# Layer phase: GpSimd's rotation behind VectorE's, value sums two head pairs at a time, statistics and second parts moved to the residual

## The reference, cut to what matters

```python
xn = _layernorm(x, axis=-1)
# first block: 16 heads of 16, segments of 512 tokens, keys and values of every eighth token
q, k, v = (qkv[0] * scale, qkv[1], qkv[2])
scores = jnp.einsum('bhspd,bhskd->bhspk', q4, k4).reshape(B, H, S, nb, BLOCK_M, Kn)
c = jnp.max(scores, axis=4, keepdims=True)
w = jnp.exp(scores - c)
den = jnp.sum(w, axis=-1) + 1e-10
out = jnp.einsum('bhsnmk,bhskd->bhsnmd', w, v4) / den[..., None]
s = out @ Wout.T
g = _silu(quantised(xn) @ weight.T + bias)
x = x + s * g
# second block
xn = _layernorm(x, axis=-1)
q = rope(xn @ wq + bq); k = rope(xn @ wk + bk); v = xn @ wv + bv
# causal attention per head, then a mixture of 8 experts as the gate, x = x + s * g
```

## Time and profile before

| what | value |
|---|---|
| the profiled execution's own time | 3820.8 us |
| span of its instructions | 3819.0 us |
| median of the three timed runs | 3812.4 us |
| busy share of the span: PE, DVE, ACT, POOL | 85%, 72%, 52%, 17% |
| mean granted TensorE clock, share of full speed | 0.92 |
| iterations 2 to 14 of the layer phase, 148.81 to 886.18 | 737.4 us |

### The profile page before, as it was taken

One profiled execution on the slowest core, in us unless ns is written; L12 is line 12 of the kernel. 1 busy time (PEld: TensorE's weight loads), 2 busy tenths in 40 slices (PEclk: granted clock), 3 DMA queues, 4 the chain that ended last, 5 costly groups with the idle time before them and its releaser, 6 DMA issues. The chain is left out here.

```text
span 3819.0 us, 67859 instructions
## 1 busy us (share of the span) xinstructions
PE 3249.5 (85%) x22678; PEld 1773.4 (46%) x22679; DVE 2754.2 (72%) x5118; ACT 2004.4 (52%) x3363; POOL 651.7 (17%) x954
## 2 busy tenths in 40 slices
PE   5878878877398898899899899999979899999977
PEld 2434434434133333333333333333348788888865
DVE  5777777776778888788788888888725565555547
ACT  2333333333057777788788788788852232222224
POOL 1132222222122232000000000000023323223310
PEclk9999999998579999999999999999989999999989
DMA  2122222222422211222222112220031121111149
GB/s 72 50 71 67 61 67 67 61 67 67 86 43 46 45 19 32 47 46 45 47 46 45 21 31 46 46 46 18 17 108 63 39 78 44 59 54 45 45 131 332
DMA packets 252770, 230.55 MB, mean 60 GB/s; under 512 B 60924, under 2 KB 235132, under 8 KB 252156
## 3 DMA queue, kind: packets, MB, share of 16 engines
q1 hardware_dynamic: 236040, 192.39, 19.9%
q0 software_dynamic: 16384, 33.64, 2.8%
HBM read 124.28 MB, written 101.06 MB: 59 GB/s over the span
## 5 line engine op out<-in xcount | busy, mean ns | idle before, releaser
L1474 ACT ACTIVATE at_ex<-at_so,keep_exp_scale 128x512 f32<-128x512 f32 (+1 forms) x2304 | 1350.6, 673 | 447.9 <-PE at_so L1368 241.4
L1501 DVE TENSOR_REDUCE at_best<-at_p 128x1 f32<-128x512 f32 (+3 forms) x2560 | 1393.3, 603 | 261.4 <-PE at_p L1350 162.9
L1350 PE MATMUL at_p<-at_ks,at_qs 48*128 48x512 f16 (+3 forms) x2560 | 811.4, 370 | 165.6 <-DVE at_best L1501 123.7
L1368 PE MATMUL at_so<-at_qs,at_ks 50*128 50x512 f16 (+3 forms) x2560 | 694.5, 362 | 18.7 <-issue 9.5
L1422 PE MATMUL at_ob<-at_ex,at_vs 128*32 128x512 f32 (+3 forms) x5120 | 608.3, 567 | 0.5 <-issue 0.4
L1772 ACT ACTIVATE e_hh<-e_hb,e_b1now 128x512 fp32r<-128x512 f32 x256 | 174.5, 690 | 595.5 <-PE e_hb L1707 541.6
L1657 POOL DMA_INDIRECT e_xg<-s_xn,e_token x128 | 143.4, 1121 | 1695.7 <-DVE e_token L1802 1523.8
L1350 PEld LDWEIGHTS at_p<-at_ks,at_qs 48*128 48x128 f16 x2560 | 216.9, 94 | 459.3 <-DVE at_best L1501 393.1
L1368 PEld LDWEIGHTS at_so<-at_qs,at_ks 50*128 50x128 f16 x2560 | 200.1, 95 | 464.6 <-ACT at_ex L1474 346.4
L1737 PE MATMUL e_ob<-e_w2h,e_hh 128*128 128x256 f32 x1024 | 298.5, 292 | 15.7 <-DVE e_og L1840 15.1
L1738 PE MATMUL e_ob<-e_w2l,e_hh 128*128 128x256 f32 x1024 | 294.4, 288 | 0.0
(11 more groups left out here) (209 smaller groups left out, 4651.6 us busy)
## 6 DMA issues: line engine op xcount, KB each, us to landing
s_v<-a_v SPq DMA_DIRECT2D x64, 256.0 KB, 3.2
s_qk<-a_part SPq DMA_DIRECT2D x128, 128.0 KB, 2.4
at_vs<-s_v SPq DMA_DIRECT2D x32, 512.0 KB
s_eo<-at_empty SPq DMA_DIRECT2D x16, 1024.0 KB
e_w<-w SPq DMA_DIRECT2D x16, 1024.0 KB
f_rows<-s_eo SPq DMA_DIRECT2D x32, 512.0 KB, 8.4
at_qs<-s_qk SPq DMA_DIRECT2D x96, 128.0 KB
at_ks<-s_qk SPq DMA_DIRECT2D x96, 128.0 KB
```

The lines of the kernel that those rows point to most:

```text
L1350: last = pe.matmul(out, qs[rows, buf, p, qt * P:(qt + 1) * P], ks[rows, buf, p, ch * SEG:ch * SEG + w], start=True, stop=ch != qc)
L1368: last = pe.matmul(so[:, v % NST, at:at + w], ks[rows, r, p, kt * P:(kt + 1) * P], qs[rows, r, p, q0:q0 + w], start=True, stop=not diag)
L1474: ev.done(act.activation(ex[:, v % NE, 0:width], so[:, v % NST, 0:width], ACT.Exp, scale=keep["exp_scale"][:, 0:1]), "ex")
L1501: ev.done(dve.tensor_reduce(best[:, row:row + 1, ch], p1[:, (at + e) % NP1, 0:wide(item)], AX, ALU.max), "mx")
```

## The change

POOL's rotation waits for the end of DVE's rotation of the same segment instead of for the copies of q and k. PE's order in the pair loop is changed: the values of two pairs follow each other behind the second scores of the next two, each value waits for the exponentials of both pairs, and `wexp` has four buffers instead of two. ACT's copies to `oT` come one pair later, the first part at p = 6 instead of 3. On DVE `normalise` comes two pairs later, the second part `rest` and the statistics of the next x leave the pair loop: the statistics stand behind the second `gated`, then the multiplication of the gate, then `rest`, then the tokens xn of the next segment, then the remaining part of the residual. The number of instructions of each kind is the same.

```diff
+        NW = 4
-        wexp = sb("wexp", [P, 2, SEG])
+        wexp = sb("wexp", [P, NW, SEG])
@@ gpsimd, rotate
-                    ev.wait(pool, "pjc", n, 4)
+                    ev.wait(pool, "rot", n, 1)
@@ tensor, values
-                    ev.wait(pe, "wexp", m, p + 1)
+                    ev.wait(pe, "wexp", m, p + 2 - p % 2)
-                    ev.done(pe.matmul(ob[r:r + 2 * HW, :], vbd[:, p, :], wexp[:, p % 2, :], start=True, stop=True), "pv")
+                    ev.done(pe.matmul(ob[r:r + 2 * HW, :], vbd[:, p, :], wexp[:, p % NW, :], start=True, stop=True), "pv")
@@ tensor, the pair loop
-                        if p >= 1:
+                        if p >= 2 and p % 2 == 0:
+                            values(m, p - 2)
                             values(m, p - 1)
-                        if p >= 3 and p % 2 == 1:
-                            turn(m, (p - 3) // 2)
+                        if p >= 4 and p % 2 == 0:
+                            turn(m, (p - 4) // 2)
+                    values(m, NP0 - 2)
                     values(m, NP0 - 1)
+                    turn(m, 2)
                     gate(m, 0)
@@ scalar, the pair loop
-                        ev.wait(act, "pv", m, max(p - 1, 0))
-                        ev.done(act.activation(wexp[:, p % 2, :], shifted[:, p % 2, :], ACT.Exp, scale=SCALE), "wexp")
+                        ev.wait(act, "pv", m, max(p - NW + 1, 0))
+                        ev.done(act.activation(wexp[:, p % NW, :], shifted[:, p % 2, :], ACT.Exp, scale=SCALE), "wexp")
-                        if p == 3 and n >= 1:
+                        if p == 6 and n >= 1:
                             part0(n - 1)
-                        if p >= 2 and p % 2 == 0:
-                            out_copy(m, p // 2 - 1)
+                        if p >= 3 and p % 2 == 1:
+                            out_copy(m, (p - 3) // 2)
@@ vector, residual
-                def residual(st, m):
-
-                    ev.wait(dve, "ez", m, 2)
-                    st.mark(dve.scalar_tensor_tensor(out=z[:], in0=ez[:], scalar=1.0, in1=z[:],
-                                                     op0=ALU.add, op1=ALU.mult), "gate", m)
-                    st.settle()
+                def residual(st, m, half):
+
+                    if half == 0:
+                        ev.wait(dve, "ez", m, 2)
+                        st.mark(dve.scalar_tensor_tensor(out=z[:], in0=ez[:], scalar=1.0, in1=z[:],
+                                                         op0=ALU.add, op1=ALU.mult), "gate", m)
+                        return
+                    ev.wait(dve, "gate", m, 1)
@@ vector, the loop
-                        if p == 4 and n >= 1:
-                            rest(st, n - 1)
-                        if p >= 3 and p % 2 == 1:
-                            normalise(st, m, (p - 3) // 2)
-                        if p == 5 and more:
-                            normed_tokens(st, m + 1, 0)
+                        if p >= 5 and p % 2 == 1:
+                            normalise(st, m, (p - 5) // 2)
+                    normalise(st, m, 2)
                     gated(st, m, 0)
                     normalise(st, m, 3)
                     gated(st, m, 1)
                     if more:
+                        normed_tokens(st, m + 1, 0)
+                    residual(st, m, 0)
+                    if n >= 1:
+                        rest(st, n - 1)
+                    if more:
                         normed_tokens(st, m + 1, 1)
-                    residual(st, m)
+                    residual(st, m, 1)
                     second_norm(st, m, 0)
```

## The result

The changed kernel takes 3871.5 us (median of four runs, 3867.5 to 3880.2), the kernel before in the same comparison 3814.7 (3809.0 to 3821.1): a ratio of 1.0148 with an interval of 1.0125 to 1.0171. So it is 57 us slower, clear of the noise, where 100 were forecast; 3871 lies inside the range, 41 under the predicted number. The profiled execution of after took 3867.5 with a span of 3865.7.

What follows compares the result with a forecast made beforehand. Neither PE (82% busy) nor DVE (75%) was full, so the order of waits decides. 33.6 + 29.4 = 63.0 against 56.7 an iteration, +82 over 13; with iteration 15, tail and first iterations +100: 3912 us, range 3845 to 3950.

Steps and rivals of the forecast that it cites:

- POOL's operations block the four normalisations, in turns: Start of an iteration: POOL's three rotations alternate with the four L768; xn1 ready at 8.1 instead of 2.7.
- A: Rival at the iteration start: the four L768 keep the port together; +3.1 an iteration, +51 in total; chance 0.13.
- B: Rival at the iteration start: L768 free, L789 and L791 blocked; +1.6 an iteration, +28 in total; chance 0.10.
- C: Rival: nothing at the iteration start blocks; -1.4 or -0.7 an iteration, -14 or -4 in total; chance 0.11.
- two values 2.0: Pair loop: the value matmuls of two pairs take 2.0 on PE within a round of 6.4.
- the 32.9 of the prediction: Pair loop: the first gate matmul starts 32.9 into the iteration, before half pace is added; 26.7 before the change.
- the 0.7: Gate: added to its start time for half pace behind a 2.8 gap before values 6, making 33.6.
- the second stall: Behind the gate: Newton steps on POOL are shut out, xn comes late, PE stands 3.2 before its transpose.
- D: Rival: half pace on PE behind its 3.2 stall, 1.5 more each time, +20 to +40; upper edge of forecast's 0.60.
- taking them out of the loop gains nothing there: Pair loop: moving out L871 (2.29) and the statistics (2.4) gains nothing; the round's own chain fills the time.
- the third part: Statistics and second parts moved to the residual: 3.2 of the 3.8 gained on the rotation given back there.
- the tail: End of the layer phase: +6.4 for the last block's xn1 and +7.1 for POOL's last rotation following DVE's.

## Why the prediction was right in its sign and off in its size

**Right: POOL's operations block the four normalisations, in turns.** Shift 1 came at 7.7 into the iteration (forecast 8.0), xn1 at 7.7 (8.1), PE's gap was 5.2 (5.6), and half pace followed it. L768 was taken as a blocked form by its neighbour L703; rivals A (it goes in one piece) and B, C (it is free) fell with the 6.42. The four begin at 207.29, when L330 is half done, and the last of them ends at 213.71, half a microsecond behind POOL's L333 (213.25): 5.05 more than the 1.37 that they take alone, for three operations of POOL's.

**Wrong: "two values 2.0".** The term of the round that I priced by one pair, doubled. One pair is 1.04 and two are 1.08. It entered four times. Values 0 and 1 took 1.98 at half pace, not 3.8; the scores behind them ran at half pace too and gave part of that back, so values 2 came at 16.5, not 17.75 (0.3 of it because xn1 was ready earlier). From there to the gate 12.9 passed, not 15.2. So the gate came 3.5 earlier than the 32.9 of the prediction; the 0.7 that I added to the 32.9 is there, but inside the gate (2.24 against 1.47). With the two forced apart values 2 came at 17.76 and the rounds were 6.43. The rest of the round was sized rightly, and the rounds of 5.27 are made of it.

**Wrong by the part that I had given to a rival: the clock behind the second stall (D).** The stall itself came as worked out: statistics, two-input work on DVE, the Newton step behind L877, xn 2.96 late, PE 3.09 (forecast 3.2). Behind it the transposes took 1.66 where they take 1.04 at full pace, and L500 3.04 where it takes 1.88: +1.8 an iteration. I had 0.60 on the forecast with D as its edge; in all thirteen iterations of after it is simply part of it. Together: 63.0 - 3.5 + 1.8 = 61.3, the iteration of the trace. That the total came within 41 us of the forecast is in part luck, since these two errors have opposite signs. Nor is the 1.8 a fixed price: with the values forced apart a stall of 3.11 at the same place was followed by full pace in one iteration (1.09 and 1.88, at 395.89) and by half pace in the next (1.97 and 2.40, at 460.23).

**The mean is lower, 60.9, by two iterations.** Those that start at 390.00 and 693.69 are 58.3 long. The same gap of 2.75 precedes their last values, and these and the gate run at full pace (granted clock 1.00):

```profile
415.69 1.08 PE L444 MATMUL a_ob<-a_wexp,a_vbd 128*64 128x512 f32 x4 [2.75 <-ACT a_oT L583]
...
417.19 1.47 PE L462 MATMUL a_pb<-a_wf_piece,a_xq 128*128 128x256 bf16 x12
```

So a gap of 2.75 was followed by half pace in some iterations (1.52 and 2.24 in the fence above) and not in others, and the two kinds differ by 3.0 us: 2.2 up to the gate and 0.8 in it. In its first half the short kind is at half pace for the transposes and for a part of values 0 and 1 and the scores behind them alone. I had half pace on the first values and 0.7 at the gate, in all iterations alike. The kinds follow a rhythm: the first halves of iterations 2 to 6 are 29.51, 29.43, 29.34, 29.23 and 27.19, and those of 7 to 11 29.42, 29.33, 29.24, 29.15 and 27.24. What sets it is not shown. Iteration 15 is of the short kind, 27.2 up to its gate where 33.6 was forecast, and that is 6.4 of the 7.7 that it lacks of its +6.4.

**Wrong: "taking them out of the loop gains nothing there".** The statistics alone were worth 1.9 in the loop with pairs, and the two moves 3.7 with single values. I had argued from the round's chain, which the shifts are part of: an instruction on DVE that isn't in the chain is still in front of a shift that is. The sum is not touched by it, since the forecast of the rounds already left the two out, but the third part taken by itself was misjudged: not nothing gained and 3.2 lost, but 3.7 gained and 3.6 lost, even at 0.9991.

**Right: the tail.** It grew by 11.6 (13.5). The last xn1 took 7.51, not 1.37: +6.1, against 6.4. The difference to the 13.5 is mostly half pace that before had in its tail and after has not (L499 9.89 against 9.07, the last L517 1.98 against 1.13). POOL's last rotation, which starts only when DVE's is over, is +7.2, against the 7.1 of the prediction: part 0 starts 12.1 before the end of the phase in both kernels, behind L865 before (963.29 + 1.22) and behind POOL in after, whose last operation ends 7.1 behind DVE's:

```profile
1022.39 2.34 POOL L333 TENSOR_TENSOR a_rot<-a_rot,a_prod 128x1024 f32<-128x1024 f32 x1
```

Iterations 0 and 1 gained 5.6, where 1.5 was forecast; they have no blocked start, and the short rounds are in them too. I didn't take this apart further.

**How the parts add up.** Alone on before they are +1.3 (rotation), +1.3 (pairs, with part 0 at pair 3) and -0.1 (moves) an iteration, 2.5 together; the change costs 4.2. What they interact by is not taken apart; the last stall of each half is a different one in each kernel, and half pace hangs on it. The sum of single experiments would have missed the size by two fifths.

## What to carry to other kernels

When two engines lock each other out, look not only at the two operations that collide today but at every instruction that the blocked engine has behind the new start: here a rotation moved out of the way by 3.8 us cost 5.3 on four small normalisations, and one wait further on, beside shifts that read PSUM, it lengthened none of them and turned +1.5% into -0.8%. A step taken out of a loop pays in full only if its new place has no consumer waiting: the statistics at the residual put twelve dependent small steps in front of PE at a point where PE had been the limit. And a chain of small matmuls is to be priced by what stands next to it: two of 64 columns to different halves of the output, next to each other in PE's order, cost as much as one (1.08 and 1.04).

## What the runs showed that I had not expected

Two matmuls of 128x64 by 512 columns in f32, to different partitions of one PSUM tile, took 1.08 together and 2.23 when the second had to wait for the first. Copy_predicated with 1024 columns went from 1.23 to 3.25, and a compare (is_big) from 0.68 to 1.79, beside POOL's tensor_tensor; shifts with one operand in PSUM kept their 0.69. Half pace behind a stall of some 3 us at a point where PE is the limit cost 1.8 us; a gap of 2.75 in the loop and one of 3.11 before the transposes were each followed by either pace. Some kernels kept one rhythm (58.02 to 58.10 with the rotation's wait alone, 54.61 to 54.79 with POOL behind the quantisation), while others alternated between several, by up to 4.4 us from one iteration to the next, so that only the mean over all thirteen can be compared. The whole program differed by 2.6% between chips (3725.6 and 3822.0 for the same kernel before), against which the end of the layer phase gave a steadier measure.
